# A fused transformer block on Trainium2: the score maxima from 32-row tiles of the array, and the causal mask added by VectorE

## The chip, the cores and the metric

The kernel runs on one NeuronCore of a Trainium2 chip. Its five engines run beside each other and meet through semaphores: TensorE (PE in the profile, its weight loads PEld), VectorE (DVE), ScalarE (ACT), GpSimd (POOL) and SyncE (SP), which issues the DMAs. The metric is the device time of one execution in microseconds (us), lower is better. The granted TensorE clock is given as a share of 2.4 GHz.

## The reference

A transformer block on x of shape (4, 1024, 512), in fp32:

```python
# attention: 16 heads of 32
kqv = (layernorm(x) @ Wqkv + bqkv).reshape(b, s, 3, 16, 32)
q, k, v = kqv[:, :, 0], kqv[:, :, 1], kqv[:, :, 2]
scores = einsum('bsnh,btnh->bnst', k, q) / sqrt(32)
scores = triu(scores) + -10000.0 * tril(ones, k=-1)
attn = softmax(scores, axis=2)
out = einsum('bnkq,bknh->bqnh', attn, v).reshape(b, s, 512) @ Wo + bo
x = x + layernorm(out)
# FFN 512 -> 2048 -> 512 with int weights: silu(gate) * up, then down
x = x + layernorm(ffn(layernorm(x)))
```

What matters here: each query's softmax runs over the keys up to its own place (causal), and the kernel subtracts a maximum per query and head before the exponential. That number need not be the exact maximum: whatever is subtracted cancels in the quotient of numerator and denominator.

## The kernel before, in words

**Three parts.** A prologue loads and scales the weights, normalises the first batch and computes its first projections. Then attention runs over 16 groups (n = 0 to 15, `NG`), each the four heads of one 128-row slice of one batch (n = 4·batch + slice). Then the FFN runs over 8 tiles of 512 tokens.

**The order.** `order_of_jobs` (L57) writes one list of jobs, `PLAN`. Every engine walks this list and does its own share of each job, so each engine's order is fixed by it, and semaphores do the rest. Attention of group n has 12 steps (`STEPS`, L27): query half j = 0 with key blocks 0 to 3, then j = 1 with key blocks 0 to 7. A step has four `score` jobs (one per head, L612), and then, for the step before it, `num` (L622, numerator, `L634`) and `den` (L636, denominator, `L644`), which accumulate in two PSUM banks of their own. Between these the planner puts other jobs, spread over the steps by `spread` (L93): `qk` of group n + 2 in steps 0 to 3, `mjob` of group n + 1 over steps 3 to 9 with `mjoin` as the last item, `mturn` in step 10; `vproj` in the groups with n mod 4 of 2 and 3; the layer norm of the next batch (`ln1`) where n mod 4 is 1; the output projection, residual and second norm of the batch before (`wo`) where n mod 4 is 0 and n > 0. Within a step the jobs of all these are cut into four pieces (L141 to L151).

**Score maxima.** `max_lots` (L38) lists 38 lots per group: a lot is one to four products of a block of 128 queries with 128 to 512 keys of one head, written to one PSUM bank; 22 of them have their last 128 keys on the diagonal of the causal mask. TensorE does a lot at L592 to L606: per product one matmul over 96 rows of the packs (three fp16 products of high and low halves), and on the diagonal a second matmul of 128 columns (L604) that adds the mask, `low` times `id16`. VectorE takes the maximum of the lot with one `tensor_reduce` (L863 to L874) into `mcol`. `mjoin` (L875) combines the two parts of the later queries, `mturn` turns the maxima (L611), VectorE splits them into two fp16 rows (L881 to L890), and SyncE writes these rows by DMA into rows 96 and 97 of the query pack (L471). So each score matmul of group n (98 rows) subtracts the maxima itself.

**Packs and stages.** ScalarE writes the high half of q and k (L734) and a full copy (L738), GpSimd the low half (L1031), both in `stage`, four heads on 32 partitions each. SyncE then issues 24 DMAs per group (`packs`, L461 to L470) that put the halves of each head under each other. Before, an `mjob` waits for those 24 (L596).

**PSUM banks.** Six banks rotate (L211 to L229): every job that writes PSUM takes the next bank and waits until the last user of it has been read (`emptied`, L383). A lot takes one bank.

Of the kernel before, what the change touches and what calls it, by code (L numbers as in the profile page):

```python
# [8 lines left out]
F16 = mybir.dt.float16  # L9
BF16 = mybir.dt.bfloat16  # L10
# [27 lines left out]
def max_lots():  # L38

    lots = []  # L40
    for first in (0, 512):
        lots.append([(h, first // 128, first, 128) for h in range(4)])
        for h in (0, 2):
            lots.append([(h, first // 128 + 1, first, 256), (h + 1, first // 128 + 1, first, 256)])
        for h in range(4):
            lots.append([(h, first // 128 + 2, first, 384)])
            lots.append([(h, first // 128 + 3, first, 512)])
    for h in range(4):
        for qb in range(4, 8):
            lots.append([(h, qb, 0, 512)])  # L50
    return lots
# [5 lines left out]
def order_of_jobs():  # L57
# [29 lines left out]
    for i in range(len(LOTS)):  # L87
        add(("mjob", 0, i))
        if i % 4 == 2 and fill:
            add(fill.pop(0))  # L90
# [122 lines left out]
for job in PLAN:  # L213
    if job[0] in ("ln1_turn", "turn2", "norms", "qk", "vproj", "mjob", "mturn", "score", "woproj"):
        uses = [job]
    elif job[0] == "gate_up":
        uses = [("gate", job[1]), ("up", job[1])]
    else:
        continue
    for use in uses:  # L220
        if use == ("gate", 0):
            turn = 0
        size = 4 if ("gate", 0) in BANK or use == ("gate", 0) else 6
        BANK[use] = turn % size
        FORMER[use] = held.get(turn % size)
        held[turn % size] = use
        turn += 1
        if use == ("gate", 0):
            LEFT = dict(held)  # L229
# [30 lines left out]
def build(nc, x, wqkv, bqk, bqkv, wo, bo, wg, wu, gs, us, wd, ds, out):  # L260
    ctx = ExitStack()
    with ctx:
# [44 lines left out]
        ident = A("ident", [128, 128], F32)  # L307
        id16 = A("id16", [128, 128], F16)
        low = A("low", [128, 128], F16)
        ones = A("ones", [128, 32], F32)  # L310
# [72 lines left out]
        def emptied(use):  # L383

            kind = use[0]
            if kind in ("gate", "up"):
                return {"gate": s_sg, "up": s_hf}[kind], use[1] + 1
            return {"ln1_turn": s_xl, "turn2": s_x2l, "norms": s_cmax, "qk": s_tq, "vproj": s_vw, "mjob": s_mr,
                    "mturn": s_mf, "score": s_ex, "woproj": s_yt}[kind], NO[use]

        def N_(a, b):
            return nrm[:, a:b]

        c_v, c_o, esc, beta = N_(34, 35), N_(35, 36), N_(36, 37), N_(21, 22)

        def rawof(m):
# [145 lines left out]
        def _(pe):  # L542
# [8 lines left out]
            for job in PLAN:  # L551
# [9 lines left out]
                elif kind == "norms":  # L561
                    m = a[0]
                    e.wait_ge(s_const, 8)
                    e.wait_ge(s_sq, NO[job])
# [27 lines left out]
                elif kind == "mjob":  # L592
                    n, i = a
                    qp, kp = packs[n % 2]
                    e.wait_ge(s_const, 6)
                    e.wait_ge(d_p[n % 2], packed(n))  # L596
                    bk = bank(job)
                    at = 0
                    for h, qb, k0, w in LOTS[i]:
                        diag = k0 + w == (qb + 1) * 128  # L600
                        mm = pe.matmul(bk[:, at:at + w], qp[0:96, h, qb * 128:(qb + 1) * 128],  # L601
                                       kp[0:96, h, k0:k0 + w], start=True, stop=not diag)
                        if diag:
                            mm = pe.matmul(bk[:, at + w - 128:at + w], low[:], id16[:], start=False, stop=True)  # L604
                        at += w
                    mm.then_inc(s_mx, 1)  # L606
                elif kind == "mturn":
# [28 lines left out]
                elif kind == "den":  # L636
                    n, j, kb = a
                    ks = (STEP[a] - 1) % 2
                    off = max(0, kb - 4 * j) * 128
                    e.wait_ge(s_const, 7)  # L640
                    if kb == 0 and (n, j) != (0, 0):
# [50 lines left out]
        def _(act):  # L692
            e = Engine(act)
            for job in PLAN:
# [30 lines left out]
                elif kind == "qk":  # L725
# [47 lines left out]
        def _(dve):  # L773
# [14 lines left out]
            for job in PLAN:  # L788
# [74 lines left out]
                elif kind == "mjob":  # L863
                    n, i = a
                    h0, qb, k0, w = LOTS[i][0]
                    nh = len(LOTS[i])
                    col = h0 * 8 + qb if k0 == 0 else 32 + h0 * 4 + qb - 4
                    step = 8 if k0 == 0 else 4
                    if n >= 2:
                        e.wait_ge(s_mt, NO["mturn", n - 2])  # L870
                    e.wait_ge(s_mx, NO[job])
                    dve.tensor_reduce(mcol[:, n % 2, col:col + step * (nh - 1) + 1:step],  # L872
                                      ps[:, BANK[job], 0:nh * w].rearrange("p (h k) -> p h k", h=nh), AX.X, ALU.max
                                      ).then_inc(s_mr, 1)  # L874
                elif kind == "mjoin":  # L875
                    n = a[0]
                    of_all = mcol[:, n % 2, 0:32].rearrange("p (h q) -> p h q", h=4)[:, :, 4:8]
                    e.wait_ge(s_mr, len(LOTS) * (n + 1))
                    dve.tensor_tensor(of_all, of_all, mcol[:, n % 2, 32:48].rearrange("p (h q) -> p h q", h=4), ALU.max
# [90 lines left out]
        def _(pool):  # L970
# [4 lines left out]
                               pattern=[[-1, 128]], channel_multiplier=1).then_inc(s_const, 1)  # L975
            pool.memset(id16[:], 0.0).then_inc(s_const, 1)
            e.wait_ge(s_const, 3)
            pool.affine_select(out=id16[:], in_=id16[:], compare_op=ALU.not_equal, fill=MROW, base=0,
                               pattern=[[-1, 128]], channel_multiplier=1).then_inc(s_const, 1)
            pool.memset(low[:], 0.0).then_inc(s_const, 1)  # L980
            e.wait_ge(s_const, 5)
            pool.affine_select(out=low[:], in_=low[:], compare_op=ALU.is_ge, fill=-65504.0, base=0,
                               pattern=[[1, 128]], channel_multiplier=-1).then_inc(s_const, 1)
            pool.memset(ones[:], 1.0).then_inc(s_const, 1)
# [4 lines left out]
            def deviation(job, scale):  # L989

                no = STAT[job]
                m = (no - 1) % 6
                e.wait_ge(s_mv, no)
                pool.tensor_scalar(rs[:, m, 0:1], mv[:, m, 1:2], EPS, scale ** -2, ALU.add, ALU.mult).then_inc(s_var, 1)  # L994
                e.wait_ge(s_const, 10)
                e.wait_ge(s_var, no)
                pool.tensor_tensor(rs[:, m, 1:2], rs[:, m, 0:1], half[:, 0:1], ALU.pow).then_inc(s_rs, 1)

            for job in PLAN:
# [7 lines left out]
                elif kind == "norms":  # L1007
# [3 lines left out]
                                       ).then_inc(s_pn, 1)  # L1011
                    e.wait_ge(s_const, 10)
                    e.wait_ge(s_pn, pn(m, 1))
# [77 lines left out]
```

## Time and profile before

| | us |
|---|---|
| Median of 3 runs | 1866.24 (1865.65 to 1867.76) |
| The profiled execution's own time | 1863.75 |
| Span of the profiled execution, first to last instruction | 1862.0 |
| Prologue / attention / FFN in it | 114.9 / 1035.9 / 711.2 |
| PE busy | 1719.7 (92%) |
| DVE busy | 1062.0 (57%) |
| ACT busy | 716.1 (38%) |
| POOL busy | 332.4 (18%) |
| Granted clock, mean | 0.971 |

The own time less the span, 1.75 us, lies around the instructions. PE's busy time overlaps with itself: a matmul starts while the one before it still drains, so a matmul costs the distance to the next start, not its duration. The same holds in small for VectorE: an instruction can start some 0.08 us before the last one's recorded end.

### The profile page before, as it was taken

To read this page: it belongs to the slowest core of one execution; us is meant where nothing else is said; L and a number is where in the kernel's file an instruction comes from. 1 tells how busy PE (TensorE), PEld (TensorE's weight loads), DVE (VectorE), ACT (ScalarE), POOL (GpSimd) and SP (SyncE) were. 2 spreads that over 40 slices of the span, in tenths; PEclk is the share of its full clock that TensorE was granted. 3 is DMA by queue.
4 is the path that set the end of the run, shared out by engine and by line. 5 is a ranking of instruction groups with operands and counts; after the bars stand their busy time and mean duration, and the time that the engine had idled before them with its cause. 6 is when DMAs were issued, how large, how long until landed. Compare 5 with 4: busy or idle time off the path is not lost.

```text
span 1862.0 us, 25259 instructions
## 1 busy us (share of the span) xinstructions
PE 1719.7 (92%) x10015; PEld 782.5 (42%) x10016; DVE 1062.0 (57%) x1779; ACT 716.1 (38%) x1271; POOL 332.4 (18%) x558
## 2 busy tenths in 40 slices
PE   3889899998899989899989788999999999999997
PEld 1433333343333333233333223555555555555554
DVE  5545864685864686765695576724343333434254
ACT  3335555444555445555435454222222222222221
POOL 2212222133222223222222133100000000000000
PEclk7989999999999999899999989999999999999999
DMA  5111111122111222101222255311010100101000
GB/s 175 35 35 36 37 44 35 47 74 86 51 31 35 59 70 78 51 19 35 69 68 69 58 189 161 120 35 45 23 46 29 40 35 34 40 30 39 29 23 23
DMA packets 59174, 104.17 MB, mean 56 GB/s; under 512 B 11440, under 2 KB 11440, under 8 KB 59056
## 3 DMA queue, kind: packets, MB, share of 16 engines
q1 hardware_dynamic: 59056, 102.56, 18.3%
q8 instruction: 79, 1.29, 0.3%
q14 instruction: 39, 0.32, 0.1%
HBM read 51.92 MB, written 25.17 MB: 41 GB/s over the span
## 4 chain that ended last, share of the span: by engine, by line
PE 72%; DVE 16%; ACT 3%; issue 3%; DMA 2%; SPq 2%; POOL 1%; DVEq 0%; ACTq 0%; POOLq 0%
PE ps L669 24%; PE ps L686 13%; PE ps L578 8%; PE ps L634 6%; PE ps L644 6%; DVE mcol L872 5%; PE ps L601 4%; PE ps L620 4%; PE ps L589 4%; DVE st L779 2%; PE ps L655 2%; SPq L469 2%; DVE rec L900 2%; ACT pt L748 1%; PE ps L559 1%
## 5 line engine op out<-in xcount | busy, mean ns | idle before, releaser
L748 ACT ACTIVATE pt<-ps,nrm 128x512 f32<-128x512 f32 (+3 forms) x768 | 389.5, 584 | 363.7 <-PE ps L620 363.4
L669 PE MATMUL ps<-x2in,gu 128*128 128x512 f16 x2048 | 463.9, 380 | 0.0
L872 DVE TENSOR_REDUCE mcol<-ps 128x1 f32<-128x512 f32 (+3 forms) x608 | 357.4, 650 | 141.0 <-PE ps L604 128.4
L669 PEld LDWEIGHTS ps<-x2in,gu 128*128 128x128 f16 x2048 | 190.8, 98 | 244.4 <-issue 31.6
L601 PE MATMUL ps<-kpack,qpack 96*128 96x512 f16 (+3 forms) x768 | 218.3, 333 | 47.9 <-DVE yt L910 17.9
L944 DVE SCALAR_TENSOR_TENSOR hf<-ps,usc,sg 128x512 f32<-128x512 f32 x128 | 96.2, 751 | 270.0 <-PE ps L669 268.7
L686 PE MATMUL ps<-wd,hh 128*128 128x512 f32 x512 | 224.0, 438 | 0.0
L620 PE MATMUL ps<-qpack,kpack 98*128 98x512 f16 (+3 forms) x768 | 201.3, 335 | 18.5 <-DMA qpack<-mt 8.2
L686 PE MATMUL ps<-wd,hl 128*128 128x512 f32 x512 | 200.7, 392 | 0.0
L994 POOL TENSOR_SCALAR rs<-mv 128x1 f32<-128x1 f32 x128 | 26.3, 205 | 921.5 <-DVE mv L781 921.5
L634 PE MATMUL ps<-pt,v 128*32 128x512 f32 (+3 forms) x1536 | 172.4, 522 | 17.4 <-DVE atf L896 14.8
L770 ACT ACTIVATE hh<-hf 128x512 fp32r<-128x512 f32 x128 | 81.0, 633 | 264.5 <-DVE hf L944 250.9
L765 ACT ACTIVATE sg<-ps,gsc 128x512 f32<-128x512 f32 x128 | 87.8, 686 | 244.8 <-PE ps L669 244.8
L644 PE MATMUL ps<-pt,ones 128*32 128x512 f32 (+3 forms) x1536 | 168.2, 511 | 0.0
L601 PEld LDWEIGHTS ps<-kpack,qpack 96*128 96x128 f16 x768 | 73.4, 98 | 188.6 <-ACT pt L748 55.0
L947 DVE TENSOR_TENSOR hl<-hf,hh 128x512 fp32r<-128x512 f32 x128 | 89.0, 696 | 97.2 <-ACT hh L770 97.2
L620 PEld LDWEIGHTS ps<-qpack,kpack 98*128 98x128 f16 x768 | 59.2, 99 | 175.9 <-issue 92.9
L900 DVE RECIPROCAL rec<-rec 128x128 f32<-128x128 f32 x128 | 112.9, 920 | 11.6 <-ACT rec L755 11.6
L1038 POOL TENSOR_SCALAR_AFFINE_SELECT pt<-pt 128x512 f32<-128x512 f32 x128 | 82.7, 646 | 205.7 <-ACT pt L748 205.7
L686 PEld LDWEIGHTS ps<-wd,hh 128*128 128x128 f32 x512 | 96.4, 188 | 30.8
L686 PEld LDWEIGHTS ps<-wd,hl 128*128 128x128 f32 x512 | 96.4, 188 | 20.0
L1031 POOL TENSOR_TENSOR stage<-tq,stage 128x512 f16<-128x512 f32 x64 | 74.6, 1166 | 148.5 <-ACT tq L738 148.5
(103 smaller groups left out, 1622.8 us busy)
## 6 DMA issues: line engine op xcount, KB each, us to landing
qpack<-stage SPq DMA_DIRECT2D x192, 64.0 KB, 2.0
kpack<-stage SPq DMA_DIRECT2D x192, 64.0 KB, 2.0
xin<-in_x SPq DMA_DIRECT2D x32, 256.0 KB, 2.6
xr<-in_x SPq DMA_DIRECT2D x32, 256.0 KB, 2.9
x1d<-x SPq DMA_DIRECT2D x32, 256.0 KB, 3.2
x2d<-x2s SPq DMA_DIRECT2D x32, 256.0 KB, 2.0
x2in<-x2d SPq DMA_DIRECT2D x8, 1024.0 KB, 5.6
x1in<-x1d SPq DMA_DIRECT2D x8, 1024.0 KB, 5.7
```

The source lines that it names most:

```text
L578: mm = pe.matmul(bk, W[w][:, c, f:f + 128], xT[q][:, c, j * 512:(j + 1) * 512], start=i == 0 and c == 0, stop=i == 2 and c == 3)
L601: mm = pe.matmul(bk[:, at:at + w], qp[0:96, h, qb * 128:(qb + 1) * 128], kp[0:96, h, k0:k0 + w], start=True, stop=not diag)
L620: pe.matmul(bk[:, off:512], kp[0:98, h, kb * 128:(kb + 1) * 128], qp[0:98, h, j * 512 + off:(j + 1) * 512], start=True, stop=True).then_in ...
L634: pe.matmul(NUM[32 * h:32 * h + 32, off:512], V[b % 2][:, kb, g * 128 + 32 * h:g * 128 + 32 * h + 32], Pt[:, ks, h, off:512], start=kb == ...
L644: mm = pe.matmul(DEN[32 * h:32 * h + 32, off:512], ones[:], Pt[:, ks, h, off:512], start=kb == 0, stop=kb == 4 * j + 3)
L669: mm = pe.matmul(bk, GU[:, c, m, i * 128:(i + 1) * 128], x2in[:, 1 - k, :, p, c, :], start=p == 0 and c == 0, stop=p == 1 and c == 3)
L686: mm = pe.matmul(ps[:, 4 + s, :], src[:, n % 4, s * 128:(s + 1) * 128], WD[:, i, :], start=i == 0 and p == 0, stop=i == 15 and p == 1)
L748: act.activation(Pt[:, (step - 1) % 2, h, off:512], ps[:, BANK[job], off:512], ACT.Exp, scale=esc).then_inc(s_ex, 1)
L872: dve.tensor_reduce(mcol[:, n % 2, col:col + step * (nh - 1) + 1:step], ps[:, BANK[job], 0:nh * w].rearrange("p (h k) -> p h k", h=nh), AX ...
L900: dve.reciprocal(rec[:, c * 128:c * 128 + 128], rec[:, c * 128:c * 128 + 128]).then_inc(s_iv, 1)
L944: dve.scalar_tensor_tensor(out=hf[:, n % 2, :], in0=ps[:, BANK["up", n], :], scalar=usc[:, i:i + 1], in1=sg[:, n % 2, :], op0=ALU.mult, op ...
L947: dve.tensor_tensor(hl[:, n % 4, :], hf[:, n % 2, :], hh[:, n % 4, :].bitcast(F32), ALU.subtract).then_inc(s_hl, 1)
```

## The change

- **Operands.** The product of a lot now uses only the high halves, straight from `stage`: head h lies on partitions 32h to 32h + 31, so the four heads' products, 32 rows each, go to four row tiles of the array (`tile_position=(32h, 0)`). It waits for ScalarE's high halves, no longer for the pack DMAs.
- **Lots.** A lot is now all four heads of one block of queries and one range of keys: 12 lots per group (8 on the diagonal, 4 full ones of 512 keys) in place of 38. It takes four banks in turn, one per head. `spread` gives two lots to each of steps 3 to 8, and `mjoin` to step 9. In the prologue one filling job follows every second lot.
- **Mask.** The second matmul is gone. VectorE reads a diagonal product with `tensor_tensor_reduce`: it adds `low` (bf16, 0 or -1e30), writes the sum back to the same PSUM bank and gives the maximum. Full products keep `tensor_reduce`. That is 32 + 16 = 48 VectorE instructions per group for 38, over the same 18,432 columns.
- **Constants.** `id16` is gone and `low` is four times as wide; two GpSimd instructions fewer at the start.

```diff
@@ max_lots
     lots = []
-    for first in (0, 512):
-        lots.append([(h, first // 128, first, 128) for h in range(4)])
...
+    for qb in range(8):
+        if qb >= 4:
+            lots.append((qb, 0, 512))
+        first = qb // 4 * 512
+        lots.append((qb, first, (qb + 1) * 128 - first))
     return lots
@@ order_of_jobs
-        if i % 4 == 2 and fill:
+        if i % 2 == 1 and fill:
@@ the rotation of banks
+    elif job[0] == "mjob":
+        uses = [("max",) + job[1:] + (h,) for h in range(4)]
@@ build
-        id16 = A("id16", [128, 128], F16)
-        low = A("low", [128, 128], F16)
+        low = A("low", [128, 512], BF16)
...
+        def reduced(n, i, h):
+            return 4 * (len(LOTS) * n + i) + h + 1
@@ TensorE, mjob
-                    qp, kp = packs[n % 2]
-                    e.wait_ge(s_const, 6)
-                    e.wait_ge(d_p[n % 2], packed(n))
-                    bk = bank(job)
-                    at = 0
-                    for h, qb, k0, w in LOTS[i]:
-                        diag = k0 + w == (qb + 1) * 128
-                        mm = pe.matmul(bk[:, at:at + w], qp[0:96, h, qb * 128:(qb + 1) * 128],
-                                       kp[0:96, h, k0:k0 + w], start=True, stop=not diag)
-                        if diag:
-                            mm = pe.matmul(bk[:, at + w - 128:at + w], low[:], id16[:], start=False, stop=True)
-                        at += w
-                    mm.then_inc(s_mx, 1)
+                    stage = stages[n % 2]
+                    qb, k0, w = LOTS[i]
+                    e.wait_ge(s_qh, NO["qk", n, 0, qb // 4])
+                    e.wait_ge(s_qh, NO["qk", n, 1, (k0 + w - 1) // 512])
+                    for h in range(4):
+                        bk = bank(("max", n, i, h))
+                        rows = slice(32 * h, 32 * h + 32)
+                        pe.matmul(bk[:, 0:w], stage[rows, 0, 0, qb * 128:(qb + 1) * 128], stage[rows, 1, 0, k0:k0 + w],
+                                  start=True, stop=True, tile_position=(32 * h, 0)).then_inc(s_mx, 1)
@@ ScalarE, qk
                     if n >= 2:
                         e.wait_ge(d_p[n % 2], packed(n - 2))
+                        e.wait_ge(s_mx, reduced(n - 2, len(LOTS) - 1, 3))
@@ VectorE, mjob
-                    dve.tensor_reduce(mcol[:, n % 2, col:col + step * (nh - 1) + 1:step],
-                                      ps[:, BANK[job], 0:nh * w].rearrange("p (h k) -> p h k", h=nh), AX.X, ALU.max
-                                      ).then_inc(s_mr, 1)
+                    e.wait_ge(s_const, 4)
+                    for h in range(4):
+                        bk = ps[:, BANK["max", n, i, h], 0:w]
+                        e.wait_ge(s_mx, reduced(n, i, h))
+                        if k0 + w == (qb + 1) * 128:
+                            col = h * 8 + qb if k0 == 0 else 32 + h * 4 + qb - 4
+                            dve.tensor_tensor_reduce(out=bk, in0=bk, in1=low[:, 512 - w:512], scale=1.0,
+                                                     scalar=-1e30, op0=ALU.add, op1=ALU.max,
+                                                     accum_out=mcol[:, n % 2, col:col + 1]).then_inc(s_mr, 1)
+                        else:
+                            col = h * 8 + qb
+                            dve.tensor_reduce(mcol[:, n % 2, col:col + 1], bk, AX.X, ALU.max).then_inc(s_mr, 1)
```

## Rows read from the trace of the kernel before

**Rows 1.** The page, busy time of each engine.
```profile
PE 1719.7 (92%) x10015; PEld 782.5 (42%) x10016; DVE 1062.0 (57%) x1779; ACT 716.1 (38%) x1271; POOL 332.4 (18%) x558
```

**Rows 2.** Busy time by stretch: stretch, length, each engine (instructions), clock, DMA share, GB/s.
```profile
0.00:114.90 114.90, 69.38 (x320) 33.34 (x322) 67.86 (x121) 36.25 (x46) 24.54 (x58) 0.84 0.28 85
114.90:1150.80 1035.90, 952.38 (x6497) 355.25 (x6498) 689.79 (x1178) 504.14 (x955) 269.80 (x406) 0.97 0.22 62
1150.80:1862.00 711.20, 697.92 (x3200) 393.92 (x3199) 304.37 (x481) 175.66 (x270) 38.08 (x94) 0.99 0.12 42
```

**Rows 3.** The same view, steps 3 to 9 of groups 3, 5, 8, 13, 14.
```profile
311.30:348.80 37.50, 36.99 (x260) 13.53 (x256) 29.13 (x48) 17.86 (x33) 7.71 (x9) 1.00 0.00 1
460.20:501.90 41.70, 36.06 (x256) 14.02 (x252) 36.72 (x68) 20.88 (x38) 12.41 (x21) 0.96 0.15 38
655.10:709.60 54.50, 47.68 (x320) 20.15 (x316) 50.08 (x89) 21.51 (x39) 14.71 (x28) 1.00 0.22 70
1010.60:1043.70 33.10, 31.66 (x236) 11.31 (x232) 27.49 (x46) 17.93 (x33) 7.72 (x9) 1.00 0.05 11
1056.80:1097.50 40.70, 30.09 (x224) 11.67 (x220) 29.84 (x50) 16.00 (x29) 10.55 (x12) 0.92 0.44 132
```

**Rows 4.** Timeline of PE, full-array matmuls with a mask between: start, length, instruction.
```profile
72.02 0.22 PE L601 MATMUL ps<-kpack,qpack 96*128 96x128 f16 x1
72.08 0.22 PE L604 MATMUL ps<-id,low 128*128 128x128 f16 x1
72.14 0.27 PE L601 MATMUL ps<-kpack,qpack 96*128 96x256 f16 x1
```

**Rows 5.** Timeline of PE, in and out of the four-column-tile matmuls.
```profile
613.73 0.60 PE L601 MATMUL ps<-kpack,qpack 96*128 96x512 f16 x2
614.26 1.07 PE L644 MATMUL ps<-pt,ones 128*32 128x512 f32 x8
615.26 0.60 PE L620 MATMUL ps<-qpack,kpack 98*128 98x512 f16 x2
```

**Rows 6.** The chain of waits: start, length, what.
```profile
559.88 0.99 PE ps L634 x8
...
567.44 0.57 PE ps L634 x8
```

**Rows 7.** Groups of VectorE's reduces: count, busy us, mean ns, idle before.
```profile
L872 DVE TENSOR_REDUCE mcol<-ps 128x1 f32<-128x512 f32 x384 | 245.5, 679 | 14.9 <-PE ps L601 11.0 <-PE ps L604 2.4
L872 DVE TENSOR_REDUCE mcol<-ps 128x1 f32<-128x384 f32 x128 | 70.0, 547 | 2.5 <-PE ps L604 2.5
```

**Rows 8.** L872 alone on DVE, steps 3 to 9 of group 3.
```profile
311.30:348.80 37.50, 22.53 (x38) 1.00 0.00 1
```

**Rows 9.** Timeline of DVE, three back-to-back stretches.
```profile
337.18 1.89 DVE L872 TENSOR_REDUCE mcol<-ps 128x1 f32<-128x512 f32 x3
...
678.06 0.69 DVE L779 BATCH_NORM_STATS2 st<-x 128x6 f32<-128x512 f32 x1
678.78 0.18 DVE L781 BATCH_NORM_AGGREGATE mv<-st 128x2 f32<-128x6 f32 x1
678.88 0.72 DVE L910 SCALAR_TENSOR_TENSOR yt<-ps,nrm,bo_b 128x512 f32<-128x512 f32 x1
...
693.26 0.68 DVE L809 TENSOR_TENSOR x2s<-ps,x2s 128x512 f16<-128x512 f32 x1
693.86 0.54 DVE L786 TENSOR_SCALAR xn<-x,mv,rs 128x512 f32<-128x512 f32 x1
```

**Rows 10.** Timeline of DVE, the first reduces of steps 3 to 9, group 3.
```profile
314.75 3.51 DVE L872 TENSOR_REDUCE mcol<-ps 128x4 f32<-128x512 f32 x6 [8.78 <-PE ps L604]
```

**Rows 11.** Waits in 1049.2 to 1072: total, times, longest.
```profile
PE ps L601 <- DMA kpack<-stage: 8.6, 1, 8.6
```

**Rows 12.** Timelines of DVE and PE, the end of the prologue.
```profile
110.89 0.18 DVE L879 TENSOR_TENSOR mcol<-mcol 128x16 f32<-128x16 f32 x1
...
114.92 1.86 PE L620 MATMUL ps<-qpack,kpack 98*128 98x512 f16 x4 [3.40 <-issue]
```

More of the change, by code:

```diff
@@ L40, in max_lots @@
     lots = []
-    for first in (0, 512):
-        lots.append([(h, first // 128, first, 128) for h in range(4)])
[L43 to L50, printed above, removed]
+    for qb in range(8):
[3 more added lines that the diff above has]
+        lots.append((qb, first, (qb + 1) * 128 - first))
     return lots
@@ L213 @@
 for job in PLAN:
-    if job[0] in ("ln1_turn", "turn2", "norms", "qk", "vproj", "mjob", "mturn", "score", "woproj"):
+    if job[0] in ("ln1_turn", "turn2", "norms", "qk", "vproj", "mturn", "score", "woproj"):
         uses = [job]
+    elif job[0] == "mjob":
+        uses = [("max",) + job[1:] + (h,) for h in range(4)]
     elif job[0] == "gate_up":
@@ L387, in emptied @@
                 return {"gate": s_sg, "up": s_hf}[kind], use[1] + 1
-            return {"ln1_turn": s_xl, "turn2": s_x2l, "norms": s_cmax, "qk": s_tq, "vproj": s_vw, "mjob": s_mr,
+            if kind == "max":
+                return s_mr, reduced(*use[1:])
+            return {"ln1_turn": s_xl, "turn2": s_x2l, "norms": s_cmax, "qk": s_tq, "vproj": s_vw,
                     "mturn": s_mf, "score": s_ex, "woproj": s_yt}[kind], NO[use]
@@ L562, in _ @@
                     m = a[0]
-                    e.wait_ge(s_const, 8)
+                    e.wait_ge(s_const, 6)
                     e.wait_ge(s_sq, NO[job])
@@ L639, in _ @@
                     off = max(0, kb - 4 * j) * 128
-                    e.wait_ge(s_const, 7)
+                    e.wait_ge(s_const, 5)
                     if kb == 0 and (n, j) != (0, 0):
@@ L864, in _ @@
                     n, i = a
[L865 to L868, printed above, removed]
+                    qb, k0, w = LOTS[i]
                     if n >= 2:
                         e.wait_ge(s_mt, NO["mturn", n - 2])
-                    e.wait_ge(s_mx, NO[job])
-                    dve.tensor_reduce(mcol[:, n % 2, col:col + step * (nh - 1) + 1:step],
-                                      ps[:, BANK[job], 0:nh * w].rearrange("p (h k) -> p h k", h=nh), AX.X, ALU.max
-                                      ).then_inc(s_mr, 1)
+                    e.wait_ge(s_const, 4)
[10 more added lines that the diff above has]
+                            dve.tensor_reduce(mcol[:, n % 2, col:col + 1], bk, AX.X, ALU.max).then_inc(s_mr, 1)
                 elif kind == "mjoin":
@@ L877, in _ @@
                     of_all = mcol[:, n % 2, 0:32].rearrange("p (h q) -> p h q", h=4)[:, :, 4:8]
-                    e.wait_ge(s_mr, len(LOTS) * (n + 1))
+                    e.wait_ge(s_mr, reduced(n, len(LOTS) - 1, 3))
                     dve.tensor_tensor(of_all, of_all, mcol[:, n % 2, 32:48].rearrange("p (h q) -> p h q", h=4), ALU.max
@@ L975, in _ @@
                                pattern=[[-1, 128]], channel_multiplier=1).then_inc(s_const, 1)
-            pool.memset(id16[:], 0.0).then_inc(s_const, 1)
+            pool.memset(low[:], 0.0).then_inc(s_const, 1)
             e.wait_ge(s_const, 3)
-            pool.affine_select(out=id16[:], in_=id16[:], compare_op=ALU.not_equal, fill=MROW, base=0,
+            pool.affine_select(out=low[:, 384:512], in_=low[:, 384:512], compare_op=ALU.is_ge, fill=-1e30, base=0,
                                pattern=[[-1, 128]], channel_multiplier=1).then_inc(s_const, 1)
[L980 to L983, printed above, removed]
             pool.memset(ones[:], 1.0).then_inc(s_const, 1)
@@ L994, in deviation @@
                 pool.tensor_scalar(rs[:, m, 0:1], mv[:, m, 1:2], EPS, scale ** -2, ALU.add, ALU.mult).then_inc(s_var, 1)
-                e.wait_ge(s_const, 10)
+                e.wait_ge(s_const, 8)
                 e.wait_ge(s_var, no)
@@ L1011, in _ @@
                                        ).then_inc(s_pn, 1)
-                    e.wait_ge(s_const, 10)
+                    e.wait_ge(s_const, 8)
                     e.wait_ge(s_pn, pn(m, 1))
```

## The prediction

> **What bounds the kernel now.** The page's busy times come first: PE 92%, DVE 57% [rows 1]. Cut into the three parts, the FFN is PE's alone and nothing in it changes; the change acts in the 1035.9 us of attention and at the end of the prologue [rows 2]. An average over attention (PE 952, DVE 690) hides two limits, so the next view is steps 3 to 9 of single groups, where all the lots lie [rows 3]. Group 3 takes 37.5 us with PE busy 36.99: TensorE sets the end and VectorE, 29.1, has room. Groups 2, 6, 7, 10 and 11 have the same jobs. Group 5 (layer norm; 1 and 9 are like it) takes 41.7 with PE 36.1 and DVE 36.7, and group 8 (output projection; 4 and 12) takes 54.5 with PE 47.7 and DVE 50.1: here VectorE is the busier one, and what neither fills is waiting between them. Group 13 (0 is like it) is 33.1 with PE 31.7, DVE 27.5; group 14 is 40.7 with a stall in it. The reader should see that a cheaper PE pays only where DVE has room, and that a dearer DVE costs at once where it has none.
>
> **TensorE, removed and added.** Starts, not durations: 128 columns are 0.06 us apart, the mask matmul 0.06 too [rows 4]; 512 columns are 0.22 (0.60 for two, less the 0.38 of one) [rows 5]; 256 and 384 lie on that line at 0.11 and 0.165. A group's 32 diagonal products are 8 x (0.06 + 0.11 + 0.165 + 0.22) = 4.4 us, the 16 full ones 3.5, the 32 masks 1.9: 9.8 us now. After, if the four tiles run together, a lot costs its columns once: 2 x 0.555 + 4 x 0.22 = 2.0 us. To this comes the change of array shape. No row shows row tiles; the nearest are the column tiles of `num` and `den`. Into them: two 512-column matmuls start at 613.73 and would be through at 614.17, the next starts at 614.26: 0.10 [rows 5]. Inside: 512 columns take 0.99 and 256 take 0.57, so 0.21 per 128 columns, and 0.15 are left over [rows 6]. I charge both, 0.25 a visit; 12 visits are 3.0 us. After: 5.0, a saving of **4.8 us a group**. Bounds: 7.8 saved if a visit costs nothing, and a loss of 1.1 if the tiles run one after another (7.9 + 3.0 against 9.8). I take the middle because the column tiles of the same array do run together: eight recorded matmuls of 512 columns in 0.99.
>
> The Trainium skill, "TensorE: Matmul & The Clock Gate", Part 3, gives four row tiles of 512 columns a measured 3.07 times, not 4. By that the products cost 2.6 for 2.0, and the saving would be an estimated 4.2 us.
>
> **VectorE, removed and added.** The 38 reduces of group 3 are busy 22.5 us [rows 8]. Back to back a 512-column reduce costs 0.60 ((1.89 - 0.69)/2) [rows 9] and 128 columns less cost 0.13 less (679 against 547 ns) [rows 7]. After, 16 full reduces stay: 9.6. The 32 others become add, write to PSUM and maximum in one instruction; no row shows it. Nearest row for the body: a two-operand instruction that reads PSUM and writes SBUF, 0.60 to the next start (693.26 to 693.86) [rows 9]. For handing out the maximum: at least nothing; 0.10 as the small aggregate that is followed at once (678.78 to 678.88); and, if it must wait for the body to end as the aggregate does for its statistics, 0.72 + 0.10 = 0.82 in all [rows 9]. So 0.60 below, 0.82 above, and I take 0.75, nearer the upper since the maximum is known only when the body has ended. Shorter ones lose 0.13 per 128 columns: 0.75 + 0.62 + 0.49 + 0.36 = 2.2, times 8 = 17.7. Sum 27.3 for 22.5: **+4.8 us a group**; nothing at 0.60, +7.1 at 0.82.
>
> **By group, steps 3 to 9.** Groups 5 and 8 and their four likes: VectorE sets the end, so +4.8, less some 0.8 because its inputs come earlier: 6 x 4.0 = +24. Group 3 and its five likes: PE would need 37.5 - 4.8 = 32.7, but DVE has 29.1 + 4.8 = 33.9 and can't begin before the first lot. Now it begins 3.4 us in [rows 10]; a `qk` of 12 matmuls (2.6 us) still lies ahead of that lot, so 2.9 stay, and the stretch is 36.8: 6 x -0.7 = -4. PE saves 4.8 and 0.7 is kept; what is late next is VectorE. Groups 0 and 13: 27.5 + 4.8 + 2.9 = 35.2 for 33.1: +4 together. Group 14: PE stands 8.6 us for the pack DMAs of group 15, which SyncE issues one by one [rows 11]; the new lots don't wait for packs, so the 40.7 become 32.1, and DVE's 29.8 + 4.8 = 34.6 then rule: -6. Group 15 has no lots.
>
> **Prologue.** `mjoin` ends at 111.1 and the first score starts at 114.9 [rows 12]. With six fillings among 12 lots, and two `vproj` (5.2 us) that now come after `mturn`, DVE is through some 3 us earlier, but the fillings then stand on PE before the first score: -2. The two missing GpSimd constants, the extra wait of ScalarE's `qk` on lots two groups old, and the new waits for the high halves cost nothing: each is met steps before. If that cover went, it would be the `qk` of the same group, 2.6 us, that the first lot waits for.
>
> Sum: 24 - 4 + 4 - 6 - 2 = **+16 us**. Against the profiled execution's own 1863.75 that is 1880; its runs' median is 2.5 higher, so **1882 us**.
>
> **The order of waits.** A lot takes four of six banks. TensorE issues in order, so if lot i + 1 finds its bank unread, the scores behind it wait too, and ScalarE's exponentials behind these. In stretches that VectorE sets anyway that is not a second charge; in group 3's it is how DVE becomes the limit. The Trainium skill, "TensorEngine Tiling (Array Packing)", § PSUM Bottleneck, says that tiling makes TensorE faster but not the reading of PSUM, which may become the limit. By that alone the PE saving is worth nothing; [rows 3] agree for groups 5 and 8 and leave 8.4 us of room in group 3.
>
> **Rivals.**
> 1. *The mask costs VectorE nothing (faster).* At 0.60: groups like 5 and 8 -0.8 each (-5), like 3 down to PE's 32.7 (-4.8 each, -29), 0 and 13 to 30.4 (-5), 14 -10, prologue -5: -54, **1812 us**. The two ends are 70 us apart for 0.15 us, so it decides at about 0.71: below it the change is faster. For it: a two-operand read costs no more than a reduce [rows 9]. Against: 32 results have to be handed out.
> 2. *Write-back costs a second pass.* Body and write share one bank; if they alternate, each diagonal column costs twice. Columns alone are 0.53, 0.40, 0.27, 0.13 (from the 0.13 above), 8 x 1.33 = +10.6 more: +15.4 a group. Groups like 5 and 8 +88, like 3 +59, 0 and 13 +25, the rest +14: **2052 us**. No instruction of DVE in the trace writes PSUM, so nothing speaks against it but that PSUM reads cost no more than SBUF reads. The Trainium skill, "Vector Engine (DVE) Microarchitecture Reference", § 7, has this shape of instruction at half rate when both sources are non-bf16 in SBUF; here one is PSUM and the mask is bf16, so to the letter it doesn't apply.
> 3. *Row tiles don't run together.* PE +1.1 a group: groups like 3 need 38.6, +11 over my sum: **1893 us**.
>
> **Chances.** My case 0.42; rival 1 0.35; the crossing between the two, within 0.2% (3.7 us, about what a measurement can tell from no change), 0.08; rival 2 0.07; rival 3 0.08. With 0.82 the same sum gives +53, 1919. The range runs from 1825, short of rival 1's end, to 1960, which adds room for order effects above 1919 and leaves out rival 2: some 0.2 outside. Faster 0.35, same 0.08, slower 0.42 + 0.07 + 0.08 = 0.57. The likeliest case's own range is 1870 to 1925.
>
> **What would show it.** Diagonal instructions of 512 columns 0.75 apart; DVE busy in attention up by 15 x 4.8 = 72 us; 0.45 us of PE per lot; steps 3 to 9 of group 3 near 36.8 with DVE busy over 90%, of group 8 near 58.5; no wait for packs in group 14; the FFN at 711. I am wrong if DVE in group 3's stretch has room (rival 1), or if PE per lot is near 1.1.

## The result and the profile after

The changed kernel takes **1943.28 us** (median; 1939.57 to 1943.56), against 1865.95 for the kernel before: ratio **1.041**, 95% interval 1.0392 to 1.0428. The forecast was 1882 with 0.57 for slower. The sign is the one held likeliest and the time lies within the wide range of 1825 to 1960, but outside the likeliest case's own 1870 to 1925: the loss is 77 us where 16 were summed up, nearly five times as much.

The page after, to be read against [rows 1]:

```profile
span 1941.1 us, 24921 instructions
PE 1761.0 (91%) x9504; PEld 744.3 (38%) x9504; DVE 1095.4 (56%) x2451; ACT 718.0 (37%) x1271; POOL 331.2 (17%) x556
```

PE lost 511 matmul records and yet is busier than before. The view by stretch says why (columns as in [rows 2]; first the three parts, then steps 3 to 9 of groups 3, 5, 8, 13 and 14, as in [rows 3]):

```profile
0.00:117.30 117.30, 70.53 (x289) 29.48 (x290) 69.08 (x160) 36.26 (x46) 24.42 (x56) 0.96 0.28 85
117.30:1230.00 1112.70, 992.05 (x6016) 320.82 (x6014) 721.63 (x1811) 506.07 (x955) 268.89 (x406) 0.88 0.20 58
1230.00:1941.00 711.00, 698.41 (x3208) 393.96 (x3200) 304.67 (x481) 175.69 (x270) 37.93 (x94) 0.99 0.12 42
326.70:366.60 39.90, 35.95 (x229) 10.68 (x225) 31.09 (x90) 17.93 (x33) 7.26 (x9) 0.96 0.00 1
485.00:537.10 52.10, 43.95 (x224) 12.31 (x222) 39.46 (x110) 21.05 (x38) 12.45 (x21) 0.71 0.09 26
699.80:760.20 60.40, 53.57 (x289) 19.23 (x286) 52.99 (x132) 21.52 (x39) 13.72 (x26) 0.83 0.19 62
1085.10:1120.80 35.70, 32.70 (x205) 8.25 (x202) 29.45 (x88) 18.06 (x33) 7.27 (x9) 0.86 0.00 1
1136.00:1178.30 42.30, 35.13 (x193) 8.48 (x190) 32.84 (x92) 16.41 (x29) 9.61 (x12) 0.76 0.40 124
```

Attention holds all of it: 1112.7 for 1035.9 us; the FFN is the same. In attention the granted clock is 0.88 where it was 0.97 [rows 2]. With levels of 1.0 and 0.5, that is 24% of the time at 1.2 GHz (267 us) for 6% (62 us). And VectorE's busy time rose by only 32 us, not by the 72 forecast. Neither engine is busy all the time in any of these stretches: in group 5's, DVE is busy 39.5 of 52.1 us. The time went into waiting and into a slow clock.

| Steps 3 to 9 of group | before | forecast | after |
|---|---|---|---|
| 3 | 37.5 | 36.8 | 39.9 |
| 5 | 41.7 | 45.7 | 52.1 |
| 8 | 54.5 | 58.5 | 60.4 |
| 13 | 33.1 | 35.2 | 35.7 |
| 14 | 40.7 | 34.6 | 42.3 |

VectorE's new instruction, in its timeline (start, length, instruction):

```profile
336.27 0.73 DVE L874 CUSTOM_DVE_ANT_0 ps<-ps,low 128x512 f32<-128x512 f32 x1
336.92 0.14 DVE L874 DVE_READ_ACCUMULATOR2_ANT mcol<- 128x1 f32 x1
336.92 0.73 DVE L874 CUSTOM_DVE_ANT_0 ps<-ps,low 128x512 f32<-128x512 f32 x1
337.57 0.14 DVE L874 DVE_READ_ACCUMULATOR2_ANT mcol<- 128x1 f32 x1
```

It is recorded as two, a body and a read of the accumulator, but the next body starts with that read: 0.65 us apart for 512 columns, against 0.60 for a reduce. Lot after lot on TensorE (timeline, as in [rows 5]):

```profile
329.48 0.22 PE L619 MATMUL ps<-qpack,kpack 98*128 98x128 f16 x1
329.63 0.23 PE L604 MATMUL ps<-stage 32*128 32x128 f16 x4
329.80 0.64 PE L633 MATMUL ps<-pt,v 128*32 128x256 f32 x8
...
357.55 0.34 PE L604 MATMUL ps<-stage 32*128 32x384 f16 x4
357.82 1.06 PE L643 MATMUL ps<-pt,ones 128*32 128x512 f32 x8
```

The four tiles do run together: 0.17 us for 4 x 128 columns, 0.27 for 4 x 384, that is 0.06 and 0.16 of columns and 0.11 to get out into the column tiles; getting in costs 0.09 more (329.48 to 329.63, less 0.06). A visit is 0.20, near the 0.25 charged.

So each single price was as forecast or cheaper. What was not in the sum is this, in the same view in step 5 of group 5:

```profile
497.63 0.61 PE L619 MATMUL ps<-qpack,kpack 98*128 98x512 f16 x1
498.30 0.26 PE L604 MATMUL ps<-stage 32*128 32x128 f16 x1
502.67 0.28 PE L604 MATMUL ps<-stage 32*128 32x128 f16 x1 [4.12 <-DVE mcol L879]
503.27 0.28 PE L604 MATMUL ps<-stage 32*128 32x128 f16 x1 [0.31 <-DVE mcol L879]
503.86 0.28 PE L604 MATMUL ps<-stage 32*128 32x128 f16 x1 [0.31 <-DVE mcol L879]
504.07 1.94 PE L633 MATMUL ps<-pt,v 128*32 128x512 f32 x8
505.94 1.12 PE L562 MATMUL ps<-ident,xn 128*128 128x128 f32 x4
```

The second head of a lot stands 4.1 us for a bank that VectorE hasn't read yet. Behind it on TensorE stand a numerator (L633) and the transposes of the layer norm (L562), and for those VectorE waits in turn. And the numerator then takes 1.9 us where it takes 1.0 at full clock. What VectorE loses by it shows in its own waits in the same stretch, steps 3 to 9 of group 5, before and after: the second half of the layer norm's transposed tile needs ScalarE's first, and that needs the transposes.

```profile
DVE xTl L804 <- ACT xTh L716: 0.2, 1, 0.2
```

```profile
DVE xTl L804 <- ACT xTh L715: 7.5, 5, 2.3
```

These 7.3 us are nearly all by which VectorE's idle time grew there (12.6 us for 5.0). Over the whole execution, TensorE's waits with a product of the maxima for a bank that a reduce still has to read (total, times, longest), first before, then after:

```profile
PE ps L601 <- DVE mcol L872: 10.8, 15, 1.5
```

```profile
PE ps L604 <- DVE mcol L879: 47.4, 87, 4.7
```

### The profile page after: what moved, and what is told of

Its sections match the earlier page's. It is cut to its first block, busy times and chain, and to the rows that moved or that the text cites. A ratio compares the mean times of both kernels' runs of the same rounds, so it can differ in the third digit from the quotient of the medians.

```text
span 1941.1 us, 24921 instructions
## 1 busy us (share of the span) xinstructions
PE 1761.0 (91%) x9504; PEld 744.3 (38%) x9504; DVE 1095.4 (56%) x2451; ACT 718.0 (37%) x1271; POOL 331.2 (17%) x556
## 4 chain that ended last, share of the span: by engine, by line
PE 69%; DVE 21%; ACT 3%; issue 3%; DMA 2%; POOL 1%; SPq 1%; DVEq 0%; ACTq 0%; POOLq 0%
PE ps L668 23%; PE ps L685 12%; PE ps L581 9%; DVE mcol L879 6%; PE ps L643 6%; PE ps L633 5%; PE ps L592 4%; DVE ps L874 4%; PE ps L619 4%; PE ps L654 2%; DVE st L779 2%; DVE rec L905 2%; PE ps L562 2%; PE ps L604 2%; DVE xn L786 1%
## 5 line engine op out<-in xcount | busy, mean ns | idle before, releaser
L874 DVE CUSTOM_DVE_ANT_0 ps<-ps,low 128x384 f32<-128x384 f32 (+3 forms) x512 | 234.6, 524 | 114.3 <-PE ps L604 113.9
L604 PE MATMUL ps<-stage 32*128 32x512 f16 (+3 forms) x768 | 144.0, 348 | 87.9 <-DVE mcol L879 47.4
L633 PE MATMUL ps<-pt,v 128*32 128x512 f32 (+3 forms) x1536 | 185.8, 559 | 10.5 <-DVE atf L901 9.3
L643 PE MATMUL ps<-pt,ones 128*32 128x512 f32 (+3 forms) x1536 | 185.8, 559 | 0.0
L879 DVE TENSOR_REDUCE mcol<-ps 128x1 f32<-128x512 f32 x256 | 157.2, 677 | 17.2 <-PE ps L604 17.0
L604 PEld LDWEIGHTS ps<-stage 32*128 32x128 f16 x768 | 42.1, 91 | 236.8 <-DVE mcol L879 68.2
```

The lines of the kernel that those rows point to most:

```text
L604: pe.matmul(bk[:, 0:w], stage[rows, 0, 0, qb * 128:(qb + 1) * 128], stage[rows, 1, 0, k0:k0 + w], start=True, stop=True, tile_position=(32 ...
L633: pe.matmul(NUM[32 * h:32 * h + 32, off:512], V[b % 2][:, kb, g * 128 + 32 * h:g * 128 + 32 * h + 32], Pt[:, ks, h, off:512], start=kb == ...
L643: mm = pe.matmul(DEN[32 * h:32 * h + 32, off:512], ones[:], Pt[:, ks, h, off:512], start=kb == 0, stop=kb == 4 * j + 3)
L874: dve.tensor_tensor_reduce(out=bk, in0=bk, in1=low[:, 512 - w:512], scale=1.0, scalar=-1e30, op0=ALU.add, op1=ALU.max, accum_out=mcol[:, n ...
L879: dve.tensor_reduce(mcol[:, n % 2, col:col + 1], bk, AX.X, ALU.max).then_inc(s_mr, 1)
```

## The experiments

Each ran in three rounds against the kernel before on the same chip, whose medians were 1863.0 to 1863.6 us; ratios are to that. The changed kernel's 1943.28 was measured where the kernel before took 1865.95; on the scale of these runs its ratio of 1.041 is about 1940 us, and differences from it below are taken from 1940. Several leave the mask out of the maxima, as each expectation says; what is subtracted is then a maximum over more keys.

### Queue or clock

**The row tiles four times over.** `REPEATS` is 4; only the last pass signals.

```diff
-                    for h in range(4):
-                        bk = bank(("max", n, i, h))
...
+                    banks = [bank(("max", n, i, h)) for h in range(4)]
+                    for again in range(REPEATS):
+                        for h in range(4):
...
+                            if again == REPEATS - 1:
+                                mm.then_inc(s_mx, 1)
```

> The changed kernel, but each lot's four row-tile matmuls are issued four times over into the same four banks, and only the last pass signals. This adds 3 x 2.0 us of TensorE work per group and nothing to any other engine. Theory Q (queue: a lot takes four of six banks, TensorE stands in order behind VectorE's reads, and scores, numerators and exponentials stand behind it): the extra TensorE work is paid at least in part, 1960 to 2030 us, clock near the changed kernel's 0.93. Theory C (clock: TensorE's work became so short that the granted clock falls to its lower level, and that is where the time went): the clock returns to 0.96 or more and the time falls below 1925 in spite of the extra work.

Measured: 2007.78 us, ratio 1.0769 (1.0752 to 1.0785); clock in attention 0.94. Of the 94 us of columns added (15 groups and the prologue at 5.9), 68 arrive. The clock rose from 0.88 to 0.94 and didn't repay them. The time is in Q's range and far from C's. But the edit does more than the expectation says: it takes all four banks before the first product, where the changed kernel takes one per product, and TensorE's waits for a bank after a diagonal or a full reduce grow from 51.5 to 138.4 us. So the run isn't clean, and it leaves open whether more columns alone would bring the clock back.

**The full array again.**

```diff
-                        pe.matmul(bk[:, 0:w], stage[rows, 0, 0, qb * 128:(qb + 1) * 128], stage[rows, 1, 0, k0:k0 + w],
-                                  start=True, stop=True, tile_position=(32 * h, 0)).then_inc(s_mx, 1)
+                        pe.matmul(bk[:, 0:w], qp[0:96, h, qb * 128:(qb + 1) * 128], kp[0:96, h, k0:k0 + w],
+                                  start=True, stop=True).then_inc(s_mx, 1)
```

> The changed kernel with the products as before (96 rows of the packs, full array, one after another, waiting for the packs), but still four heads and four banks per lot and the mask on VectorE. TensorE's work per group rises by 7.9 - 2.0 less the array changes, at most 5.9 us. Theory Q: the four-bank lots stay, so no gain, 1945 to 1985. Theory C: TensorE is busy again, the clock returns towards 0.97 and the time to 1890 to 1925.

Measured: 1911.12 us, 1.0258 (1.0239 to 1.0277). **29 us faster than the changed kernel with more TensorE work**, as C had it, and the clock in attention is back at 0.97:

```profile
114.90:1192.30 1077.40, 946.90 (x6020) 328.92 (x6018) 721.62 (x1811) 505.15 (x955) 268.05 (x406) 0.97 0.21 59
```

VectorE's busy time is that of the changed kernel. The same place in both kernels, step 4 of group 3, shows what happens (PE's timeline, changed kernel first):

```profile
334.62 1.07 PE L604 MATMUL ps<-stage 32*128 32x512 f16 x4 [0.19 <-ACT pt L748]
335.62 0.66 PE L633 MATMUL ps<-pt,v 128*32 128x128 f32 x8
336.21 1.89 PE L592 MATMUL ps<-wh,xTh 128*128 128x512 f16 x4
337.89 1.59 PE L592 MATMUL ps<-wh,xTl 128*128 128x512 f16 x4
339.32 1.03 PE L592 MATMUL ps<-wl,xTh 128*128 128x512 f16 x4
```

```profile
324.25 1.04 PE L605 MATMUL ps<-kpack,qpack 96*128 96x512 f16 x4 [0.19 <-ACT pt L749]
325.21 0.43 PE L634 MATMUL ps<-pt,v 128*32 128x128 f32 x8
325.57 1.04 PE L592 MATMUL ps<-wh,xTh 128*128 128x512 f16 x4
326.44 1.03 PE L592 MATMUL ps<-wh,xTl 128*128 128x512 f16 x4
327.31 1.03 PE L592 MATMUL ps<-wl,xTh 128*128 128x512 f16 x4
```

The lot ahead takes about 1.0 us in both, but not for the same reason. On the full array its four products start 0.22 apart and wait for nothing. In row tiles three start within 0.18 us and the last only when a bank has been read (the same timeline, cut closer):

```profile
335.31 0.38 PE L604 MATMUL ps<-stage 32*128 32x512 f16 x1
```

By these starts and 0.22 us for 512 columns, columns run for an estimated 0.6 us of the 1.0 in row tiles and for 0.87 of 0.96 on the full array; the merged rows show both as busy throughout. After row tiles the `vproj` behind it runs at 1.2 GHz (1.68 us per four matmuls), after 96 rows at 2.4 GHz (0.87). Step 4 is 8.40 us in the one and 6.76 in the other. The Trainium skill, "TensorE: Matmul & The Clock Gate", Part 1, says that the clock is gated by how busy the array has been; the trace agrees as far as it goes: the granted clock falls at 335.6, behind the lot with the gap, and stays at its upper level behind the lot without one. Whether the 32 rows count or only the idle time between them, this pair can't tell.

**One head, one bank per job.** The job takes one bank and one row tile; 48 jobs over steps 3 to 9.

```diff
+        for k0, w in ([(0, 512)] if qb >= 4 else []) + [(first, (qb + 1) * 128 - first)]:
+            for h in range(4):
+                lots.append((h, qb, k0, w))
...
+        uses = [("max",) + job[1:]]
```

> The changed kernel with each lot split into four jobs of one head and one bank, still in row tiles and with VectorE's mask; 48 jobs spread over steps 3 to 9. Row tiles meet less often, so TensorE's work rises by up to 6 us per group. Theory Q: a job waits for one bank only, the stretches of groups 5, 9 and 1 come back, 1870 to 1910 in all. Theory C: the 32-row matmuls are the same, the clock stays near 0.93 and the time at 1930 or more.

Measured: 1961.11 us, 1.0518 (1.0499 to 1.0538), clock 0.90 in attention. Slower still. The stretches of groups 1, 5 and 9 don't come back: 49.3, 50.3 and 50.6 us for the changed kernel's 50.1, 52.1 and 52.1 (43.2, 41.7 and 43.8 before). Taking four banks at once isn't what costs most there: Q, as I had put it, falls. What makes this run slower lies in groups 4, 8 and 12, which take 101 to 102 us each for 92 to 93.

**The lots from step 0.**

```diff
-                                list(range(3, 10))))
+                                list(range(0, 10))))
```

> The changed kernel with its 12 lots and the join spread over steps 0 to 9 in place of 3 to 9; the new lots need no packs, so nothing forbids it. VectorE is busy 4 to 5 of the 15 us of steps 0 to 2 before. Theory Q: lots move to where VectorE is free, 1800 to 1870 us. Theory C: TensorE's work is the same and as short, clock near 0.93 and at least 1910.

Measured: 1862.66 us, 0.9994 (0.9984 to 1.0004). The same kernel with its lots spread over ten steps is 77 us faster, level with the kernel before, as Q had it, though its clock in attention is only 0.92.

### Mask, tiles and lots apart

Four kernels make a square on the lots of four heads. The mask is taken from VectorE like this, and the full array as above:

```diff
-                        if k0 + w == (qb + 1) * 128:
...
+                        col = 32 + h * 4 + qb - 4 if k0 else h * 8 + qb
+                        dve.tensor_reduce(mcol[:, n % 2, col:col + 1], bk, AX.X, ALU.max).then_inc(s_mr, 1)
```

> Full array and four banks per lot, and no mask in the maxima at all: VectorE reads every product with tensor_reduce. It leaves the mask out of the maxima only; the scores' own mask stays. VectorE's maxima cost about 16 x 0.60 + 8 x (0.22 + 0.35 + 0.47 + 0.60) = 22.7 us per group, what they cost in the kernel before, and TensorE has 1.9 less. M: 1855 to 1880. Q: the four banks stay, 1890 to 1910.

Measured: 1904.29 us, 1.0235 (1.0204 to 1.0266).

> The row tiles alone: the changed kernel without VectorE's mask, which it leaves out of the maxima only. If the granted clock goes with the row tiles (theory T: the low records are three times as many with them, 98 against 34, whatever VectorE does), the clock stays at or below 0.94 and the time is 30 us above the run before this one, 1890 to 1935. If the low clock comes only of TensorE standing behind a dearer VectorE, it comes back to 0.96 and the two are equal.

Measured: 1928.17 us, 1.0353 (1.0334 to 1.0372); clock in attention 0.90.

| us | no mask in the maxima | mask by VectorE |
|---|---|---|
| full array, 96 rows | 1904.3 | 1911.1 |
| row tiles, 32 rows | 1928.2 | 1940 |

The row tiles cost 24 and 29 us, VectorE's mask 7 and 12. Neither together nor alone are they the largest part: the corner that has **neither** is 41 us above the kernel before, with 9 us more of VectorE in attention (699.3 for 689.8) and less on TensorE. What is left in it is the new list of lots. With it come the waits: TensorE's wait for a bank of maxima is 50.6 and 51.4 us on the full array, no less than the 47.4 with row tiles. T holds for these lots: the clock is low with row tiles, whatever VectorE does. (The expectation's 98 and 34 are all clock records; the low ones are 49 and 17.)

**The mask alone on jobs of one head** (the third run's lots, products as in the second):

> The mask alone: products on the full array from the packs, one head and one bank per job (48 jobs), mask added by VectorE. Against the run with the full array and four banks per lot (1911) only the lots of four heads are undone. If taking four of six banks at once costs (Q), 1870 to 1890; if VectorE's dearer reads are the cost (M: 24.9 us of maxima per group against 22.5), 1900 to 1920.

Measured: 1950.44 us, 1.0472 (1.0449 to 1.0496). Neither: 39 us above the lots of four heads. Smaller jobs make it worse, with or without row tiles. Between the two runs of one-head jobs the row tiles cost only 11 us, and here the full array too has a low clock in attention, 0.93: a low clock isn't peculiar to row tiles.

### What about the lots

**The same corner, its 12 lots over steps 3 to 9** (so far `mjoin` was spread with them and took step 9 for itself):

```diff
-            plans.append(spread([[("mjob", n + 1, i)] for i in range(len(LOTS))] + [[("mjoin", n + 1)]],
-                                list(range(3, 10))))
+            plans.append(spread([[("mjob", n + 1, i)] for i in range(len(LOTS))], list(range(3, 10))))
+            plans.append(spread([[("mjoin", n + 1)]], [9]))
```

> The run with the full array, four banks per lot and no mask in the maxima (1904), but its 12 lots spread over steps 3 to 9 in place of 3 to 8. Theory E (the 41 us that this run stands above the kernel before come of the planner's coarser placing: six steps for seven, two whole lots where five or six small ones stood): steps 6 to 8 of group 3 fall from 7.92, 4.88, 5.09 towards 7.5, 4.2, 4.7 and the time to 1885 to 1895. Theory B (it comes of the 48 bank turns per group for 38): no change, 1900 to 1908.

Measured: 1894.74 us, 1.0175 (1.015 to 1.0199). The placing is 10 of the 41 us, as E had it, but not where E put it: step 6 of group 3 falls from 7.92 to 6.82, step 9, which now has a lot, rises from 2.61 to 3.66, and the stretch keeps its length (38.8 and 38.9). The gain is in others, 2.2 us each in groups 1 and 9. The remaining 31 us can be the 48 turns, the other order of the products or the coarser jobs; this run doesn't part them.

**The kernel before without its mask matmuls.**

```diff
-                                       kp[0:96, h, k0:k0 + w], start=True, stop=not diag)
-                        if diag:
-                            mm = pe.matmul(bk[:, at + w - 128:at + w], low[:], id16[:], start=False, stop=True)
+                                       kp[0:96, h, k0:k0 + w], start=True, stop=True)
```

> The kernel before without the mask matmuls, so the maxima leave the mask out; 38 lots of one bank as before. TensorE does 1.9 us less per group, VectorE the same. Groups that TensorE bounds should keep all of it: 1863 - 6 x 1.9 - part of the rest, 1838 to 1850. If VectorE or the order of waits bounds them, 1858 or more.

Measured: 1860.26 us, 0.9987 (0.9973 to 1.0002). A miss, and a telling one: 1.9 us of TensorE taken from each of 15 groups, and 3 us in all are kept. Of the six groups that I had called bound by TensorE, 2, 3, 6, 7 and 11 go from 61.5 to 60.9 and group 10 to 62.0. Their steps 7 to 9, where no lot has a mask, don't move, and neither does step 6, where five have one. In steps 3 to 5 they keep 0.6 us of the 1.6 taken: over the whole run TensorE's waits for a bank that a reduce has to read grow from 10.8 to 14.9 us, and those for ScalarE's read of a `qk` bank from 3.3 to 10.5.

**The run before, each product in a bank of its own**, 48 lots in the old order:

```diff
-        lots.append([(h, first // 128, first, 128) for h in range(4)])
-        for h in (0, 2):
-            lots.append([(h, first // 128 + 1, first, 256), (h + 1, first // 128 + 1, first, 256)])
+        for h in range(4):
+            lots.append([(h, first // 128, first, 128)])
+        for h in range(4):
+            lots.append([(h, first // 128 + 1, first, 256)])
```

> As the run before it, but each product in a bank of its own: 48 lots for 38, in the old order over steps 3 to 9, same products and the same columns. Theory B: each turn of a bank costs, since a product of 128 keys now holds a whole bank, 1880 to 1910. Theory E: within 8 us of the run before it; VectorE's ten more instructions cost at most 10 x 0.07 us per group.

Measured: **1951.3 us, 1.0483 (1.0458 to 1.0507)**: 91 us for ten more jobs, and so ten more bank turns, per group. The same engines do the same columns, VectorE with ten more instructions a group (15 us more of busy time in attention). This is B's direction, far beyond what I had allowed it, but not all of it can be the price of turns: the run of 1894.7 us, with the same 48 turns in 12 jobs of four, stands 34 us over this run's base of 1860.3. Of the 93 us that attention grows here, 44 are in groups 4, 8 and 12, as in the other runs of one-head jobs, and the clock in attention is 0.92 for 0.97, without one row tile. The waits for a bank of maxima (as above), first without and then with the ten further turns:

```profile
PE ps L600 <- DVE mcol L869: 14.9, 19, 1.5
```

```profile
PE ps L601 <- DVE mcol L870: 52.2, 59, 4.4
```

### The lead, counted in banks

**The kernel before with five banks in rotation.**

```diff
-        size = 4 if ("gate", 0) in BANK or use == ("gate", 0) else 6
+        size = 4 if ("gate", 0) in BANK or use == ("gate", 0) else 5
```

> The kernel before with five banks in rotation in place of six; nothing else differs. If what the 48 bank turns cost is the shorter lead of TensorE over VectorE (theory L: a lead is counted in banks, so small products use it up), a ring that is one sixth shorter must cost too: 1885 to 1940. If the cost came of another thing in those runs (order of the heads, more semaphores), the kernel before should hardly notice, below 1872.

Measured: 1912.12 us, 1.0261 (1.024 to 1.0281). L holds: with every product and every instruction unchanged, one bank less in the rotation that maxima, scores, projections and transposes share costs 48.6 us. The same wait is 13 of them; it grows from 10.8 us to

```profile
PE ps L601 <- DVE mcol L873: 24.0, 20, 4.5
```

### Better than both

Two trials use what the change brought and leave what cost. The new products need no packs, so they can stand in steps 0 to 2, where VectorE is little used. There only row tiles will do; in later steps the packs are there, and the full array kept the higher clock on lots of four.

> A trial for a kernel better than both: lots spread over steps 0 to 9; the first four, in steps 0 to 2, where VectorE is free and the packs aren't there yet, in row tiles, the other eight on the full array from the packs. Theory T: the clock returns to 0.965 or more and the time is below that of all lots in row tiles at those steps (1863), 1825 to 1850. If TensorE's amount of work is what counts instead, it has 5 us more per group, and the time is 1865 to 1900.

Measured: 1842.74 us, 0.9898 (0.9883 to 0.9913), clock 0.974 over the execution. 20 us below all lots in row tiles.

> The trial with the first four lots in row tiles in steps 0 to 2 and the other eight on the full array (1843), without the mask in the maxima. VectorE does 2.2 us less per group: 1820 to 1838.

Measured: 1836.83 us, 0.9868 (0.9838 to 0.9898).

The second trial starts from the kernel before, without its mask matmuls. Its first 16 lots are the products of queries and keys 0 to 511, one head each, in row tiles (`TILED` is 16):

```diff
+            plans.append(spread([[("mjob", n + 1, i) for i in range(4 * k, 4 * k + 4)] for k in range(TILED // 4)],
+                                list(range(0, 3))))
+            plans.append(spread([[("mjob", n + 1, i)] for i in range(TILED, len(LOTS))] + [[("mjoin", n + 1)]],
                                 list(range(3, 10))))
...
+                    if i < TILED:
...
+                        pe.matmul(bk[:, 0:w], stage[rows, 0, 0, qb * 128:(qb + 1) * 128],
+                                  stage[rows, 1, 0, k0:k0 + w], start=True, stop=True,
+                                  tile_position=(32 * h, 0)).then_inc(s_mx, 1)
```

> A second trial for a better kernel: the 16 diagonal products of the first 512 keys in row tiles in steps 0 to 2, the other 27 lots as in the kernel before (full array, one bank, small products sharing a bank) over steps 3 to 9, no mask in the maxima. Theory L: in steps 3 to 9 it has 27 bank turns where the first trial had 32 and the kernel before 38, so it is below the trial's 1837: 1800 to 1832. If bank turns don't matter and only VectorE's load per step does, 1835 to 1850.

Measured: **1815.28 us, 0.9742 (0.9721 to 0.9763)**: 2.6% faster than the kernel before and 6.4% faster than the changed one. Attention is 986 us at a clock of 0.96, VectorE a little busier than before (699 us for 690):

```profile
115.00:1101.00 986.00, 909.78 (x6030) 321.62 (x6029) 699.07 (x1256) 508.41 (x959) 271.31 (x408) 0.96 0.23 65
```

It subtracts a maximum that also covers keys behind the mask. For data whose masked scores are far larger than the rest the exponentials might leave their range.

## Why the prediction was right or wrong

**VectorE, removed and added: mis-sized, to the dear side.** 0.65 us was measured for my 0.75; a group's maxima are busy 15.1 + 9.8 = 24.9 us, +2.4 and not +4.8. The row's warning was right that the accumulator is handed out separately; it overlaps with the next body. By my own sum the true price would have given about 1845 us, *faster*: with +2.4, groups like 5 and 8 +1.6, groups like 3 -3.1. So rival 1's condition came true (below 0.71), and its consequence did not. That the forecast had the right sign is luck: too dear a VectorE stood in for losses that weren't in the sum.

**TensorE, removed and added: right.** The tiles run together and a visit costs 0.20. The sum credited 0.7 of the 4.8 us saved to groups like 3, and would have credited 3.1 with VectorE's true price. Even that was too trusting: taking away 1.9 us a group in the kernel before was worth 0.2 on average.

**By group: the step that failed.** I added up each engine's work over seven steps and let the busier one set the end. That holds if TensorE may run ahead of VectorE by whole steps. It may run ahead by six banks. A ring of five instead of six costs 48.6 us. The new list, which takes 48 banks a group instead of 38, costs 41 with neither of the change's two instructions in it.

**The order of waits: the failing sentence** is "In stretches that VectorE sets anyway that is not a second charge". It is one. When TensorE stands at a full ring, what stands behind it (numerators, transposes, scores) is what VectorE and ScalarE need next, so VectorE falls idle too, as group 5's stretch showed. The diagonal products of 128 and 256 keys, which had shared 6 banks per group, now take 16. The corner with neither tiles nor VectorE's mask lost 41 us, 10 of them by giving step 9 to `mjoin` alone. That the other 31 are the price of the bank turns is argued, from the waits and from the ring of five; order and size of the jobs changed with them.

**Missing from the sum: the clock.** The stretches summed up had a clock of 0.92 to 1.00 [rows 3], and the sum kept it. The row tiles cost 24 to 29 us net of their saving, with attention at 0.88 to 0.90 where the full array has 0.96 to 0.97 on the same lots. [Rows 2] showed the prologue at 0.84, and the question whether a change to short 32-row matmuls keeps the clock wasn't asked.

**Group 14: half right.** The 8.6 us for packs are gone (step 3 is 2.5 us for 13.7), but its seven steps take 42.3, at a clock of 0.76: the same two losses ate it. **Prologue:** +2.4 for -2. **FFN:** 711, as said.

**The rivals.** A second pass for the write-back (rival 2): not so. Tiles one after another (rival 3): not so. None of them was the ring or the clock, and my range held the time because unknown order effects were given room.

In sum, of 77 us: about 41 the list of lots (more bank turns, six steps for seven), 24 to 29 the row tiles with their lower clock, 7 to 12 VectorE's mask, each known to some 4 us. What stays open: why one-head jobs cost most where the output projection runs (groups 4, 8 and 12 take 101 to 103 us in all three runs that have them, 86 to 88 before), and what in a lot of row tiles lets the clock fall, its 32 rows or the idle time that its short columns leave. Shown is only that on lots of four heads it goes with the tiles, and that one-head jobs on the full array lower it too.

## What to carry to other kernels

Count PSUM in turns of a ring, not in bytes: a small product that gets a bank of its own uses up the producer's lead over the consumer, and what a lost lead costs shows as waits of both engines, in neither one's busy time. Before crediting a saving on the busiest engine, take a like amount away in a trial; here 1.9 us a group were worth 0.2. Where a change loosens a dependency (here the packs), the gain lies in moving the work to where an engine is idle: that one line of the planner was worth 77 us in the changed kernel.

## What the runs showed that I had not expected

- VectorE's add, write back and maximum in place in PSUM runs at one pass: 0.65 us from start to start for 512 columns, 0.60 for the plain reduce.
- With lots of four heads in 32-row tiles attention had a mean clock of 0.88 to 0.90, with the same lots over 96 rows 0.96 to 0.97; one-head jobs over 96 rows had 0.92 to 0.93.
- In the kernel before, one bank of six is worth 48.6 us of 1863.6, more than all of its mask matmuls (3.4 us).
